# Local attention stage: queries projected transposed, probabilities turned by VectorE and DMAs

## The reference, cut to what matters

```python
qkv = x @ Wqkv                      # x: shifted tokens, INNER = 16 heads x 64
q = l2norm(q) * qs;  k = l2norm(k) * ksc
q = q * cos * scale + rotate_half(q) * sin * scale
k = k * cos * inv   + rotate_half(k) * sin * inv
sim  = einsum('bhwie,bhwje->bhwij', bq, bk2) * 8.0
sim  = where(mask, -max, sim)       # i < j or i > j + 32
attn = softmax(sim, -1)
out  = einsum('bhwij,bhwje->bhwie', attn, bv2)
x = out @ Wo + x
x = (a * gelu(gate)) @ W2 + b2 + x  # after a layer norm, W1 and b1
```

## Time and profile before

| | |
|---|---|
| median of 3 runs | 3386.17 us (3384.32 to 3388.98) |
| span of the profiled execution | 3389.4 us |
| PE busy | 3317.7 us (98%) |
| DVE busy | 2767.5 us (82%) |
| ACT busy | 2803.2 us (83%) |
| POOL busy | 2483.0 us (73%) |
| packets on the queue of POOL's DMAs | 31.4% of 16 DMA engines' span |
| on the queues of SP's and ACT's DMAs | 6.1% |

### The profile page before, as it was taken

How to read it: one execution, slowest core, us unless ns; L and a number is a source line. 1 busy time by engine, 2 the same in 40 slices (tenths; PEclk the granted TensorE clock), 3 DMA queues, 4 the chain that set the end, 5 groups by cost and what they waited for, 6 DMA issues and landing times.

```text
span 3389.4 us, 120739 instructions
## 1 busy us (share of the span) xinstructions
PE 3317.7 (98%) x49605; PEld 2474.5 (73%) x49605; DVE 2767.5 (82%) x5297; ACT 2803.2 (83%) x5522; POOL 2483.0 (73%) x4812
## 2 busy tenths in 40 slices
PE   8989998999999999999999999999999999999997
PEld 6777876577777777777777777777777777777776
DVE  6844445888888888888888888888888888899995
ACT  5756665688888888888888888888888888888885
POOL 4622223888888888888888888888888888888884
PEclk8999999999999999999999999999999999999999
DMA  3000001544444444445444444444444444444441
GB/s 108 3 7 9 8 9 35 102 83 84 85 91 98 94 84 82 83 94 105 88 82 83 89 94 98 85 86 83 95 102 83 85 85 92 83 89 85 89 88 41
DMA packets 200381, 260.15 MB, mean 77 GB/s; under 512 B 123161, under 2 KB 145438, under 8 KB 199838
## 3 DMA queue, kind: packets, MB, share of 16 engines
q0 software_dynamic: 55296, 201.35, 31.4%
q1 hardware_dynamic: 143820, 50.88, 6.1%
q10 hardware_dynamic: 722, 0.21, 0.0%
HBM read 23.95 MB, written 2.10 MB: 8 GB/s over the span
## 4 chain that ended last, share of the span: by engine, by line
PE 95%; DVE 2%; POOL 1%; issue 1%; DMA 1%; ACT 1%; SPq 0%; DVEq 0%; POOLq 0%
PE bank L1059 19%; PE bank L1034 17%; PE bank L1110 10%; PE bank L1187 10%; PE bank L1158 8%; PE bank L1174 6%; PE bank L1129 5%; PE bank L1051 4%; PE bank L675 2%; PE bank L1124 2%; PE bank L688 2%; PE bank L697 2%; PE bank L752 2%; PE bank L367 1%; PE bank L660 1%; PE bank L377 1%
## 5 line engine op out<-in xcount | busy, mean ns | idle before, releaser
L1348 DVE TENSOR_TENSOR R<-bank,tables 128x1024 f32<-128x1024 f32 x768 | 904.7, 1220 | 174.7 <-ACT sq L1246 167.2
L1059 PE MATMUL bank<-WA,xcT 128*128 128x512 f32 x1536 | 723.6, 593 | 3.0 <-ACT xcT L1221 2.1
L1034 PEld LDWEIGHTS bank<-ident,R 128*128 128x128 f32 x3072 | 365.0, 141 | 214.7 <-issue 201.2
L1361 DVE TENSOR_REDUCE ss<-sq 128x16 f32<-128x1024 f32 x384 | 460.1, 1198 | 0.0
L1473 POOL TENSOR_TENSOR P<-P,inv_sum 128x512 f32<-128x512 f32 x384 | 447.6, 1331 | 2.9 <-DVE inv_sum L1402 2.9
L1246 ACT ACTIVATE sq<-bank 128x512 f32<-128x512 f32 x768 | 431.3, 587 | 16.0 <-PE bank L1059 16.0
L1034 PE MATMUL bank<-ident,R 128*128 128x128 f32 x3072 | 431.2, 273 | 8.8 <-POOL R L1461 6.8
L1461 POOL TENSOR_TENSOR R<-R,rn 128x512 f32<-128x512 f32 x384 | 400.4, 1043 | 31.5 <-DMA R<-R 5.4
L1467 POOL TENSOR_TENSOR P<-P,rn 128x512 f32<-128x512 f32 x384 | 402.6, 1048 | 4.3 <-DVE P L1390 4.3
L1059 PEld LDWEIGHTS bank<-WA,xcT 128*128 128x128 f32 x1536 | 262.2, 191 | 188.9 <-issue 184.0
L1187 PE MATMUL bank<-WO,OT 128*128 128x128 f32 x3072 | 374.6, 275 | 0.0
(11 more groups left out here) (154 smaller groups left out, 6857.6 us busy)
## 6 DMA issues: line engine op xcount, KB each, us to landing
R<-R POOLq DMA_DIRECT2D x384, 512.0 KB, 5.0
WA<-in_wqkv SPq DMA_DIRECT2D x24, 256.0 KB, 2.9
ystat<-Y SPq DMA_DIRECT2D x192, 32.0 KB
ystat<-Y SPq DMA_DIRECT2D x384, 15.8 KB
ys<-Y SPq DMA_DIRECT2D x192, 32.0 KB
ys<-Y SPq DMA_DIRECT2D x384, 15.8 KB
WV<-in_wqkv SPq DMA_DIRECT2D x6, 512.0 KB, 4.0
WO<-in_wo SPq DMA_DIRECT2D x6, 512.0 KB, 4.3
```

The lines of the kernel that those rows point to most:

```text
L1034: return nc.tensor.transpose(dst, src, m.ident[:, :])
L1059: mm(b[QK_BANK[n, half]][:, :], m.xsT[:, t % 2, :], cols[:, half, :, :], start=True, stop=True)\
L1348: tt(both, src.unsqueeze(1).to_broadcast([128, 2, 16, 32]), tab.unsqueeze(2).to_broadcast([128, 2, 16, 32]), ALU.mult).then_inc(s.rotated. ...
L1361: nc.vector.tensor_reduce(m.ss[:, t % 2, 16 * n:16 * n + 16], m.sq[:, n, :].rearrange("p (h d) -> p h d", d=HD), AX.X, ALU.add)\
```

## The change

Six things change in `local`, and some preparation ahead of it.

1. Queries are projected transposed: the weights (reordered in `WQ`, so that the two halves of a head alternate by feature) are the stationary side, and the result is [feature, token]. `queries_turned` and `queries_out` go. `order_queries` makes `WQ` once a layer on ACT.
2. The queries' rotary works in that layout, with tables `q_tables` by feature; two accumulating DMAs of 64 partitions each, from odd to even partitions and back, replace the one of 128.
3. The sum of the squared queries over features is now a sum over partitions: PE's `query_lengths` with the weights `in_head` (32 columns), a copy by ACT, a turn by PE, and `query_floor` on DVE replace the DVE reduction.
4. Keys are written by the rotary with a step of two elements, in the same feature order as the queries.
5. Probabilities are no longer turned by PE and copied by ACT: DVE transposes 32x32 blocks into `Z` (two instructions per tile), and SP moves blocks with four DMAs (`probs_moved`). `Z` is filled with zeros once by POOL.
6. `values` are projected by token for all 128 rows at once, and `head_outputs` has the same count of 64x64 matmuls on the new layout.

The diff, cut to its core:

```diff
+def order_queries(nc, act, m, l):
+    act.wait_ge(m.w_in, 64 * l + 64)
+    nc.scalar.activation(m.WQ[:, l % 2, :].rearrange("p (h d z) -> p h d z", z=2, d=32),
+                         m.WA[:, l % 2, 0:INNER].rearrange("p (h z d) -> p h d z", z=2, d=32), ACT.Copy)\
+        .then_inc(m.w_q, 1)
...
+        def probs_moved(t):
+            if exists(t):
+                sp.wait_ge(s.p_turned.sem, s.p_turned.upto(0, t + 1))
+                z, done = m.Z[:, t % 2, :, :, :], s.p_moved[t % 2]
+                for bb in range(2):
+                    first, second = slice(64 * bb, 64 * bb + 32), slice(64 * bb + 32, 64 * bb + 64)
+                    sp.dma_start(z[first, :, 0, :], z[first, :, 1, :]).then_inc(done, 16)
+                    sp.dma_start(z[first, :, 2, :], z[second, :, 1, :]).then_inc(done, 16)
...
+        def queries(t, j):
...
+                for n in range(4):
+                    at = j * 512 + n * 128
+                    last = mm(b[QK_BANK[QUERIES, j]][:, n * 128:(n + 1) * 128], m.WQ[:, layer(t) % 2, at:at + 128],
+                              m.xsT[:, t % 2, :], start=True, stop=True)
+                last.then_inc(s.qk.sem, 1)
+
+        def query_lengths(t):
+            if exists(t):
+                pe.wait_ge(s.squared.sem, s.squared.upto((QUERIES, 1), t + 1))
+                at_least(pe, s.less.sem, s.less.upto(0, t - 1))
+                for v in range(2):
+                    for g in range(4):
+                        at = (4 * v + g) * 128
+                        last = mm(LENGTHS[32 * g:32 * g + 32, 0:128], m.in_head[:, v, :], m.sq[:, QUERIES, at:at + 128],
+                                  start=(v == 0), stop=(v == 1))
+                last.then_inc(s.q_lengths, 1)
+
+        def query_lengths_turned(t):
+            if exists(t):
+                pe.wait_ge(s.q_lengths_copied, t + 1)
+                turned(LENGTHS[:, 128:256], m.qlenT[:, :]).then_inc(s.q_lengths_turned, 1)
...
-                for e in range(2):
-                    last = mm(V_BANK[bb][64 * e:64 * e + 64, :], m.xsT[:, t % 2, bb * 64:bb * 64 + 64],
-                              cols[:, e, :, :], start=True, stop=True)
-                last.then_inc(s.v.sem, 1)
+                mm(V_BANK[j][:, :], m.xsT[:, t % 2, :], m.WV[:, j * 512:(j + 1) * 512], start=True, stop=True)\
+                    .then_inc(s.v.sem, 1)
...
-                pe.wait_ge(s.q_copied.sem, s.q_copied.upto(0, t + 1))
+                pe.wait_ge(s.q_added[t % 2], 32 * (t // 2) + 32)
                 pe.wait_ge(s.k_copied.sem, s.k_copied.upto(0, t + 1))
+                pe.wait_ge(s.q_floor, min(t + 2, N))
...
-                pe.wait_ge(s.p_copied.sem, s.p_copied.upto(0, t + 1))
+                pe.wait_ge(s.p_moved[t % 2], 64 * (t // 2) + 64)
...
             queries(i, 0)
             queries(i, 1)
-            queries_turned(i - 1, 0)
-            queries_turned(i - 1, 1)
             keys(i, 0)
             keys(i, 1)
             keys_turned(i - 1, 1)
+            query_lengths(i)
             ff_out(i - 8)
             keys_turned(i - 1, 0)
+            query_lengths_turned(i)
             normal_turned(i - 6)
             head_outputs(i - 4)
             values(i, 1)
             values(i, 0)
             scores(i - 1)
-            probs_turned(i - 3, 1)
-            probs_turned(i - 3, 0)
             ff_in(i - 7)
...
-            queries_out(i - 1, 1)
-            queries_out(i - 1, 0)
             keys_out(i - 1, 1)
             squares(i, KEYS, 1)
             if i == 0:
                 m.cross_tail()
+            query_lengths_out(i)
             normal_out(i - 6)
             squares(i, KEYS, 0)
...
-            probs_out(i - 3, 1)
-            probs_out(i - 3, 0)
             exponents(i - 2, 0)
             normalised(i - 5)
+            if i % TILES == 20 and i + TILES < N:
+                m.order_queries(act, i // TILES + 1)
...
+        def query_rotary(t, j):
...
+                tt(both, src.unsqueeze(1).to_broadcast([128, 2, 8, SEQ]),
+                   m.q_tables[:, layer(t), :, :].unsqueeze(2).to_broadcast([128, 2, 8, SEQ]), ALU.mult)\
+                    .then_inc(s.rotated.sem, 1)
...
+        def query_floor(t):
+            if exists(t):
+                dve.wait_ge(s.q_lengths_turned, t + 1)
...
+        def probs_turned(t, a):
+            if exists(t):
+                dve.wait_ge(s.normal.sem, s.normal.upto(a, t + 1))
+                if a == 1:
+                    at_least(dve, s.o, 2 * (t - 1))
+                blocks = m.P[:, t % 2, a * 512:(a + 1) * 512].rearrange("p (h k n) -> p k h n", k=2, n=32)
+                nc.vector.transpose(m.Z[:, t % 2, a, 1:3, :].rearrange("p k (h n) -> p k h n", n=32), blocks)\
+                    .then_inc(s.p_turned.sem, 1)
...
-            rotary(i, QUERIES, 0)
-            rotary(i, QUERIES, 1)
+            query_rotary(i, 0)
+            query_rotary(i, 1)
             statistics(i - 5)
-            squares_summed(i, QUERIES)
-            rotary(i, KEYS, 0)
-            rotary(i, KEYS, 1)
-            squares_summed(i, KEYS)
+            key_rotary(i, 0)
+            query_floor(i)
+            key_rotary(i, 1)
+            squares_summed(i)
+            probs_turned(i - 3, 1)
+            probs_turned(i - 3, 0)
             ff_added(i - 8)
...
-                pool.dma_start(m.R[:, QUERIES, 0, :], m.R[:, QUERIES, 1, :], accum_op=ALU.add).then_inc(s.q_added, 16)
+                for z in range(2):
+                    pool.dma_start(m.RQ[z:128:2, t % 2, 0, :], m.RQ[1 - z:128:2, t % 2, 1, :], accum_op=ALU.add)\
+                        .then_inc(s.q_added[t % 2], 16)
```

More of the change, by code:

```diff
@@ L835, in _ @@
             outputs_out(i - 1, 1)
+            if i == 16:
+                m.order_queries(act, 0)
     @m.vector.append
@@ L901, in inverse_deviation @@
                     .then_inc(s.rstd, 1)
+        pool.memset(m.Z[:, :, :, :, :], 0.0)
         for i in range(N + 2):
@@ L1132, in scores @@
                             last.then_inc(s.scores, 1)
-        def probs_turned(t, j):
-            if exists(t):
-                pe.wait_ge(s.normal.sem, s.normal.upto(j, t + 1))
-                if j == 0:
-                    at_least(pe, s.o_copied.sem, s.o_copied.upto(1, t))
-                else:
-                    pe.wait_ge(s.v_copied.sem, s.v_copied.upto(1, min(t + 4, N)))
-                    if t >= N - 3:
-                        pe.wait_ge(s.xn_copied, t - 2)
-                for n in range(4):
-                    at = j * 512 + n * 128
-                    last = turned(PT_BANK[j][:, n * 128:(n + 1) * 128], m.P[:, t % 2, at:at + 128])
-                last.then_inc(s.p_turned.sem, 1)
         def ff_in(t):
@@ new lines, in key_rotary @@
+        def key_rotary(t, half):
+            if exists(t):
+                dve.wait_ge(s.squared.sem, s.squared.upto((KEYS, half), t + 1))
+                if half == 0:
+                    at_least(dve, s.k_turned.sem, s.k_turned.upto(0, t))
+                dst = m.RK[:, 0, half:half + 1]
+                both = bass.AP(dst.tensor, dst.offset, [dst.ap[0], [1025 if half == 0 else 1023, 2], [64, 16], [2, 32]])
+                src = b[QK_BANK[KEYS, half]][:, :].rearrange("p (h d) -> p h d", d=32)
+                tab = m.tables[:, layer(t), half, :, :]
```

217 lines of the change are left out of this document (119 added, 98 removed).

## The result

The changed kernel takes 3701.9 us (median of 4 runs, 3699.5 to 3706.6) where the kernel before takes 3387.4 beside it: a ratio of 1.093, with a 95% interval of 1.092 to 1.095. It is slower by 314 us (the spans of the two profiled executions differ by 315.4); the forecast was 3630, 244 slower, with 3540 to 3860 as the range.

The account below looks back on a forecast made before the run. PE's own work bound the kernel (14.45 us a stage), a 13.52 ring through bank 7 right behind; 13.52 + 2.13 = 15.65, expected 15.7; 188 x (15.70 - 14.45) = +235, with +6 on 3389.4: 3630 us, range 3540 to 3860.

Parts of the forecast that it names:

- Transposes: Two DVE block transposes ahead of `ff_added`, priced 0.61 us each, 1.22 together, added to the path through bank 7.
- Lengths: PE's sixteen `query_lengths` instructions with 32-column weights, priced 0.60 us including 0.06 for changing over.
- Turned lengths: One more turned tile on PE (`query_lengths_turned`), priced 0.11 us, a fifth of the 0.55 for five.
- Signs: Expected: stage 15.7, DVE waiting 2 us or more at L1403, PE idle about 2 us at L1209, PE 84% busy.
- the ring through `ff_in`: Path where `ff_in` waits for `ff_added` behind the transposes, then output projection and queries on PE: 15.45 us a stage.
- the first ring: Loop from DVE's `less_maximum` freeing bank 7 through PE's keys, ACT's square, DVE's key rotary: 13.52 us before, 15.65 after.
- the other ring: Same as the first ring: the loop through bank 7, forecast at 15.65 us a stage and expected to bind.
- The rival: TensorE's clock falls after PE's new 2.1 us gap: 3853 us if every stage, 3740 if every second; chance 25%.
- the +6 for `order_queries`: Five ACT copies of 1,024 columns in the stage, 1.1 us each, on the path: +6 us in all.
- the four more issues: SP's four more transfers per tile, 0.52 us or a little more each to issue: at most 0.3 late, hidden in DVE's wait.
- Rival 4: The engines' work, not the ring of waits, decides: a stage of 13.6 us, 3232 us in all; chance 4%.
- ACT is no bound: Four ACT copies of 512 columns go (some 2.2 us), a 128-column copy comes; PE waits none, or 0.1.

Follow-up runs that it names:

- e3: The changed kernel with one more DVE reduction (0.6 us) per tile, ahead of the key rotary where DVE waits for ACT's square: 3698.1 us.
- e4: The changed kernel with one more DVE reduction (0.6 us) per tile, behind the key rotaries and ahead of the keys' sum: 3885.5 us.
- e1: The changed kernel with ACT squaring the lower key half before the lengths' copy and normal_out instead of behind them: 3528.5 us.
- e10: e9 with two Newton steps instead of three for the reciprocal lengths on POOL: 3339.6 us, ratio to before 0.987.
- e2: The changed kernel with ff_in's wait for y moved ahead of its third part, and the rotated keys' wait to its second: 3642.9 us.
- e5: The changed kernel reordered: both key squares first on ACT, key sum before key rotary on DVE, ff_in's wait split, y before layer input on SP: 3445.4 us.
- e9: e5 with ACT's copy of the second half of the values moved ahead of the two head-output copies: 3341.6 us, ratio to before 0.988.
- e7: The changed kernel with only the queries' part; probabilities, values and head outputs as in the kernel before: 3552.1 us.
- e11: e7 with ACT's exponents of the first half moved ahead of the two copies of turned probabilities: 3479.7 us.

## Why the prediction was right, and where it was off

**What bounds it.** Right in kind: PE's own work was replaced by a path over three engines with DVE's wait at the key rotary, released by ACT's lower key square, and PE idle ahead of `ff_in`. e3 against e4 shows that it is a path and not an amount of work; e1 shows that this wait closes it.

**Terms that held.** Transposes: 1.21 for the two against 1.22. Lengths: 0.57 against 0.60. Turned lengths 0.11 (six turns 0.67, five 0.55 in the earlier trace rows). The keys' rotary at its old 1.22. DVE's and POOL's work: 12.94 and 12.74 in the stage, against 13.1 and 12.8.

**Signs.** The waits came where they were forecast and a little shorter: DVE's at L1403 is 1.90, not 2 or more (2.3 in the sum), PE's at L1209 is 1.83, not 2.1. PE is busy for 88% and not 84%: its work is 14.0 in the stage, not 13.2.

**The term that was mis-sized: PE's durations behind a change of tile shape, and behind a gap.** I took rows of before as they stood. `ff_out` behind the 32-column lengths takes 0.86, not 0.67; the keys, which no longer follow another group of 512 columns but come behind the 0.13 of issue, 1.95, not 1.72; `ff_in` 1.57, not 1.33. The rows had it already: in the earlier trace rows four keys behind a wait took 1.98, where the earlier trace rows has 1.72, and in the earlier trace rows eight turns took 1.02 behind the 64x64 scores and 0.87 behind the queries. From key start to key rotary this makes 5.50 for 5.26: 0.23 + 0.19 - 0.03, and 0.16 less in ACT's part (1.01 for 4.55 - 3.38 = 1.17).

The Trainium skill ("TensorEngine Tiling (Array Packing)", section "Key Properties") says that changing the tiling mode drains TensorE. I had put 0.06 for it. The runs agree with the rule and give it a size in this kernel: a full-size group directly behind a tiled one took 0.19 to 0.20 more, `ff_out` 0.86 for 0.67, `ff_in` 1.53 for 1.33 (e10, with no wait ahead of it), the values 1.91 for the 1.72 of four such instructions. No run separates a drain from another cause that comes with the change of tile shape.

**The step that failed: which ring is first.** I put the ring through `ff_in` at 15.45, 0.2 short of the other. It came out at 15.97, since 0.24 for `ff_in`, 0.14 between `ff_added` and PE's start, 0.13 ahead of the keys and 0.05 for `ff_added` were missing from it; 0.56 in all, on a sum that gives 15.42 before rounding. I gave the hand-over from DVE to PE a price of 0.06 in the first ring and none in the second.

**Luck in the other ring.** The sum for bank 7, 15.65, is near the 15.72 that e2 shows, but its terms aren't. In e2, where no wait stands inside DVE's part, the key start to the key rotary is 5.51 and not 5.26, the key rotary to the end of `less_maximum` 10.07 and not 8.91 + 0.2 + 1.22 = 10.33 (the floor takes 0.08 of the 0.2), and the hand-over 0.15 and not 0.06. The errors cancel. In the changed kernel the same stretch on DVE lasts 10.32, because PE's output projection comes late (0.16). Likewise `ff_added` ends 10.46 behind the key start, against 10.4, with 5.50 for 5.26 on PE and ACT and 4.96 for 5.10 on DVE.

**The sum of the miss.** I forecast a stage of 15.70 and it is 15.97, because the ring through `ff_in` is the one in front: 188 x 0.27 = 51 of the 72 us between forecast and measurement.

**The clock.** The rival was right as a mechanism and far too large in size: 16 stages of 188, not all or half of them, 26 us. With the 4 us of y's transfer, forecast and runs fit together: 3630 + 51 + 26 + 4 = 3711, 6 above the span; the +6 for `order_queries` isn't seen, and four of the five stages that hold it last 15.97.

**SP.** In the steady stage the four more issues didn't bind, as forecast: from 1500 to 2300 us DVE waits for y's transfer in 15 of some 50 stages, mostly where it would have waited for the key square anyway. But I left the weight loads in SP's queue out of the sum. Where one of them waits for the end of a layer, DVE's wait reaches 3.8: twice in the changed kernel, with a stage 1.9 longer, and three times in e1, with one 3.0 longer.

**ff_in's other wait.** The circle that bound e1 and e5, through ACT's copy of the values, is in none of my lists. It was some 0.9 behind the one that binds (15.97 against the 15.06 of e1), and neither the chain of waits nor the totals of the kernel before show it.

**Rival 4 (the engines decide).** It came out at 14.1 in e9 and e10, not at 13.6, and only after five edits of order. PE's work was 13.2 in my sum; with keys +0.23, issue +0.13, `ff_out` +0.19, values +0.19 and `ff_in` +0.20 it is 14.1. The 3232 were never there: the lowest time measured is 3340.

**ACT.** "ACT is no bound" is true of its sum. Its order is another matter: e1, e7 with e11, and e5 with e9 each turned on one ACT instruction that stood behind copies that were needed later than it was; 173, 72 and 104 us.

## What to carry to other kernels

Where one engine is full, ask before moving work off it which circle over the other engines stands right behind, and price the new instructions by whether they lie on it: here 1.9 us of removed PE work bought nothing as the change stood, and 2.1 us of new work on the circle cost 1.5 a stage. Write down all the circles within half a microsecond, with every hand-over priced alike, since the nearest one may be the bound. And when such a change fails, look at the order of the in-order queues before the change is thrown away: moving a few steps, with the work unaltered, took the time from 3702 to 3342.

## What the runs showed of the hardware

- The clock is granted unevenly at one and the same pattern. With a gap of 1.83 us in nearly every stage a lower clock was granted in 16 of 188 stages (13 behind 1.83, one behind 2.06, two behind 2.19, each after a late transfer of y), with gaps of 2.43 (e4) in 62, and with the gap split into 0.63 and 0.86 (e2) in none. In no run did it hit every stage. The places aren't random either: in e4 it is nearly always every third stage, 51.2 us apart, and in the changed kernel five of the fifteen distances are 225.3, fourteen stages.
- Sixteen matmuls with 32-column weights over 128 columns took 0.57 us, against 1.79 for sixteen at full width: a factor of 3.1 for four column groups; with the 0.19 that the next group pays, 2.4.
- VectorE's block transpose of 128x512 f32 takes 0.685 us, the same as the other instructions of 512 elements: no cheaper, no dearer.
- The clock's cost isn't only in the engine that slows down: of 2.77 against 1.57 for `ff_in` and 2.33 against 1.95 for the output projection, 1.2 + 0.4 us, all came back as DVE's wait, 1.80 instead of 0.16, since both stand on the circle.
